# A gated delta-rule layer with its normalisation factor applied behind the output projection instead of ahead of it

## The reference, cut to what matters

```python
qkvz = hidden_states @ W_qkvz
conv = _silu(sum((xp[:, j:j + Tv, :] * conv_w[:, j] for j in range(CONV_K))))
# recurrence over time, per batch element and value head:
S = S * a_t[..., None, None]
err = jnp.einsum('bhkv,bhk->bhv', S, k_t)
v_new = (v_t - err) * b_t[..., None]
S = S + k_t[..., None] * v_new[..., None, :]
o = jnp.einsum('bhkv,bhk->bhv', S, q_t)
# behind it:
og = o * _silu(z)
og = og * jax.lax.rsqrt(jnp.mean(og * og, axis=-1, keepdims=True) + EPS) * norm_weight
return og.reshape(Bv, Tv, VDIM) @ W_out
```

## Time and profile before

| | us |
|---|---|
| median of 3 runs | 1351.96 |
| lowest, highest | 1344.74, 1357.4 |
| the profiled execution's own time | 1348.03 |
| its span (first to last instruction) | 1346.0 |
| busy PE, DVE, ACT, POOL | 1203.4, 924.2, 829.4, 744.7 |

### The profile page before, as it was taken

How to read it: one execution, slowest core, us unless ns; L and a number is a source line. 1 busy time by engine, 2 the same in 40 slices (tenths; PEclk the granted TensorE clock), 3 DMA queues, 4 the chain that set the end, 5 groups by cost and what they waited for, 6 DMA issues and landing times. The chain is left out here.

```text
span 1346.0 us, 30471 instructions
## 1 busy us (share of the span) xinstructions
PE 1203.4 (89%) x10744; PEld 1019.1 (76%) x10744; DVE 924.2 (69%) x2304; ACT 829.4 (62%) x2289; POOL 744.7 (55%) x1187
## 2 busy tenths in 40 slices
PE   7888998999999999999999999999998787997886
PEld 6787787787878888878877888878877676765654
DVE  6886877787878787887778787878772423325663
ACT  6335666666667676766666767667675535217773
POOL 2285756667676758585857667676757301112201
PEclk9776999999999999999999999999997869999997
DMA  4214041413121222214040403121123120001000
GB/s 168 74 38 106 6 104 7 105 24 87 31 80 35 75 41 71 53 58 103 7 107 5 106 20 91 27 83 36 36 41 108 30 94 1 0 27 41 2 9 24
DMA packets 143430, 72.82 MB, mean 54 GB/s; under 512 B 116744, under 2 KB 132624, under 8 KB 141360
## 3 DMA queue, kind: packets, MB, share of 16 engines
q1 hardware_dynamic: 143280, 70.89, 20.7%
HBM read 57.06 MB, written 13.78 MB: 53 GB/s over the span
## 5 line engine op out<-in xcount | busy, mean ns | idle before, releaser
L1011 POOL TENSOR_TENSOR tmp<-Dm,Tn 64x31 f32<-64x31 f32 (+15 forms) x496 | 262.4, 529 | 89.4 <-DMA Dm<-blk_in_scratch 54.1
L1014 POOL TENSOR_TENSOR Tn<-Tn,tmp 64x31 f32<-64x31 f32 (+15 forms) x496 | 285.4, 575 | 38.9
L823 DVE SCALAR_TENSOR_TENSOR cv<-bank,cw,cv 128x255 f32<-128x255 f32 (+2 forms) x384 | 155.2, 474 | 78.0 <-ACT cv L629 78.0
L987 POOL TENSOR_TENSOR ro<-ss,mhalf 128x4 f32<-128x4 f32 x64 | 65.1, 1017 | 250.1 <-ACT junk L691 214.0
L823 DVE SCALAR_TENSOR_TENSOR cqk<-bank,cw,cqk 128x255 f32<-128x255 f32 (+2 forms) x384 | 154.9, 473 | 7.5 <-ACT cqk L629 7.5
L454 PE MATMUL bank<-wo,OTs 128*128 128x256 f32 x512 | 138.6, 405 | 10.8 <-ACT OTs L722 10.8
L883 DVE SCALAR_TENSOR_TENSOR BP<-bank,cj,E 128x512 f32<-128x512 f32 (+1 forms) x256 | 142.8, 611 | 2.7 <-DVE cj L868 0.5
L691 ACT ACTIVATE junk<-og 128x129 f32<-128x129 f32 x256 | 79.9, 312 | 97.3 <-issue 80.6
L887 DVE TENSOR_TENSOR R<-Vs,bank 128x256 f32<-128x256 f32 x64 | 27.0, 421 | 141.9 <-PE bank L420 138.3
L454 PEld LDWEIGHTS bank<-wo,OTs 128*128 128x128 f32 x512 | 93.1, 197 | 25.8 <-ACT OTs L722 14.2
L699 ACT ACTIVATE ogn<-og,ro 128x128 f32<-128x128 f32 x256 | 81.9, 398 | 29.5 <-POOL ro L987 29.5
(11 more groups left out here) (210 smaller groups left out, 3492.7 us busy)
## 6 DMA issues: line engine op xcount, KB each, us to landing
rvz<-in_L_attn_W_qkvz SPq DMA_DIRECT2D x16, 512.0 KB, 5.0
x<-alpha_scratch SPq DMA_DIRECT2D x8, 1024.0 KB, 6.4
alb<-alpha_scratch SPq DMA_DIRECT2D x7, 1024.0 KB, 6.4
rqk<-in_L_attn_W_qkvz SPq DMA_DIRECT2D x16, 256.0 KB, 2.6
wo<-in_L_attn_W_out SPq DMA_DIRECT2D x16, 256.0 KB
blk_in_scratch<-BP SPq DMA_DIRECT2D x256, 16.0 KB, 1.5
tinv_scratch<-Tn SPq DMA_DIRECT2D x32, 128.0 KB, 2.1
tinv_t_scratch<-Tt SPq DMA_DIRECT2D x32, 128.0 KB, 2.2
```

The costliest lines, as they stand in the source:

```text
L823: nc.vector.scalar_tensor_tensor(d, bk[:, t * T:(t + 1) * T - s], cw[p][:, first + t, TAPS - 1 - s:TAPS - s], d, ALU.mult, ALU.add).then_i ...
L1011: pool_step_done(nc.gpsimd.tensor_tensor(t, Dm[:, j, j + 1:BLK].unsqueeze(2).broadcast_to([SLOTS, r, c]), Tn[:, j, 0:c].unsqueeze(1).broad ...
L1014: pool_step_done(nc.gpsimd.tensor_tensor(Tn[:, j + 1:BLK, 0:c], Tn[:, j + 1:BLK, 0:c], t, ALU.subtract), kh * NTS + 2 * j + 4)
```

## The change

1. The scaling `act_ogn` and its tile are gone. PE turns og itself. The projection writes each value head's product to its own half of the PSUM bank, for one block of 128 tokens at a time (c = 0, 1), so it is done in two rounds through the same bank; `dve_acc` takes a round with two instructions of 256 columns, each acc = product x ro + acc. The second round of the projection waits for the first round's accumulation. `ro` is now waited for by `dve_acc`.
2. The order of a step is written anew on PE, ACT and DVE.
3. The second layer: the last residual, statistics and norm of the first layer's end move from the block's boundary into the second layer's loop (k = 1, 3, 5), the first v product moves behind the first scores, and the value products are placed between turns.

```diff
             def pe_ot(kh, p, b, scaled):
-                wait(nc.tensor, "ogn", at(kh, b, 4, 4))
+                wait(nc.tensor, "og", at(kh, b, 2, 2))
...
             def pe_f(kh, p, b, c):
...
+                wait(nc.tensor, "acc", at(kh, b, 4, 2 * c))
                 for h in range(R):
-                    last = nc.tensor.matmul(bF[:, c * D:(c + 1) * D], OTs[:, h, c, :], wo[p][:, h, :],
-                                            start=(h == 0), stop=(h == R - 1))
-                if c == 1:
-                    last.then_inc(sem("f"), 1)
+                    last = nc.tensor.matmul(bF[:, h * D:(h + 1) * D], OTs[:, h, c, :], wo[p][:, h, :], start=True, stop=True)
+                last.then_inc(sem("f"), 1)
...
                 else:
+                    pe_ot(*last, 2 * (now + 2))
                     pe_solve(kh, p, b, 0)
                     pe_behind_solve(kh, b)
+                    pe_f(*last, 0)
                     if vt:
-                        pe_vt(*vt, now - 1)
+                        pe_vt(*vt, now)
...
                     pe_before_ot(kh, b)
-                    pe_ot(*last, 2 * (now + 3))
+                    pe_f(*last, 1)
                     pe_solve(kh, p, b, 2)
...
-                    pe_f(*last, 0)
-                    pe_f(*last, 1)
...
-            def act_ogn(kh, p, b):
...
+            def dve_acc(kh, p, b, c):
+                wait(nc.vector, "f", at(kh, b, 2, c + 1))
+                wait(nc.vector, "ro", at(kh, b, 1, 1))
+                a = acc[:, NC * b + c, :]
+                for h in range(R):
+                    wait(nc.vector, "acc", at(kh, b, 4, c * R + h))
+                    nc.vector.scalar_tensor_tensor(a, bF[:, h * D:(h + 1) * D], ro[b % 2][:, c * R + h:c * R + h + 1], a,
+                                                   ALU.mult, ALU.add).then_inc(sem("acc"), 1)
...
                 if not merges(b):
+                    dve_acc(*last, 0)
                     dve_r2(kh, p, b)
...
+                    if taps is taps_qk and not merges(b):
+                        dve_acc(*last, 1)
...
                 else:
+                    act_ots(*last)
                     act_y(kh, p, b, 0)
                     if vt:
                         act_vs(*vt)
-                    act_ogn(*last)
...
                     act_y(kh, p, b, 1)
-                    act_ots(*last)
...
-                res_ffn(B - 1)
-                dve.wait_ge(sem("res0b"), B)
```

More of the change, by code:

```diff
@@ L443, in pe_ot @@
                         n = h * NC + c
[L444 removed]
+                        last = nc.tensor.transpose(bOT[:, n * P:(n + 1) * P], og[b % 2][:, c, h, 0:DK], ident)
                 last.then_inc(sem("ot"), 1)
@@ L595, in pe_step @@
                     pe_solve(kh, p, b, 1)
-                    if vt:
-                        pe_vt(*vt, now)
+                    if last:
+                        pe_f(*last, 1)
                     pe_solve(kh, p, b, 2)
@@ L1313, in _ @@
                 pe_ot(NKH - 1, 1, B - 1, 2 * NG)
[L1314 to L1317, removed]
+                for m in range(2, HT):
                     pe_gate_up(0, m)
+                    if m < 4:
+                        pe_f(NKH - 1, 1, B - 1, m - 2)
                 pe_ln_turn(2)
@@ L1796, in _, with first_v @@
             def _(act):
[L1797 to L1808, removed]
+                for m in range(KC):
+                    act.wait_ge(sem("first_mm"), 2 + 2 * m)
+                    nc.scalar.activation(kp[:, m, 0:T], bank[5 - 2 * m][:, 0:T], ACT.Copy).then_inc(sem("first_act"), 1)
+                def first_v():
+                    act.wait_ge(sem("first_mm"), 5)
+                    act.wait_ge(sem("v10"), 1)
+                    for c in range(NC):
+                        for par in range(2):
+                            last = nc.scalar.activation(v1_out(0, c, 0, NH1, par), v1_in(bank[6][:, c * D:(c + 1) * D], par), ACT.Copy)
+                    last.then_inc(sem("first_act"), 1)
                 def exponents(n):
@@ L1848, in _ @@
                 for m in range(KC):
[L1849 to L1854, removed]
+                    for kind, bk in zip("qk", (4 + 2 * m, 5 - 2 * m)):
+                        product(bank[bk][:, 0:T], kind, m, slice(0, T)).then_inc(sem("first_mm"), 1)
                 pe.wait_ge(sem("first_dve"), 1)
-                pe.wait_ge(sem("first_act"), 2)
+                pe.wait_ge(sem("first_act"), KC)
                 def scores(n):
@@ L1946, in _ @@
                         pieces(k)
-                    if k == 1:
+                    if k == 0:
                         pe.wait_ge(sem("first_dve"), KC)
-                        pe.wait_ge(sem("first_act"), KC + 1)
+                        for c in range(NC):
+                            last = product_v(bank[6][:, c * D:(c + 1) * D], c, 0, D)
+                        last.then_inc(sem("first_mm"), 1)
+                    if k == 5:
+                        pe.wait_ge(sem("attn"), 1)
                         ln_turn(pe, 2, B - 1, (6, 6))
@@ L1955, in _ @@
                     if 0 <= k - 1 < NG:
-                        for j in range(GR):
+                        for j in range(2):
                             turned(GR * (k - 1) + j)
@@ L1959, in _ @@
                         values(k - 2)
-                        if k % 2 == 1:
-                            spread((k - 2) // 2)
+                    if 0 <= k - 1 < NG:
+                        for j in range(2, GR):
+                            turned(GR * (k - 1) + j)
+                    if 0 <= k - 2 < NG and k % 2 == 1:
+                        spread((k - 2) // 2)
                     if k >= 6 and (k - 6) % 4 == 0:
```

81 lines of the change are left out of this document (39 added, 42 removed).

## The result

| | before | after |
|---|---|---|
| median, us | 1349.78 (4 runs, 1344.74 to 1357.4) | 1496.37 (4 runs, 1492.65 to 1497.15) |
| profiled execution: its time, its span | 1348.03, 1346.0 | 1495.59, 1493.5 |
| mean granted clock of PE | 0.948 | 0.911 |

The ratio is 1.1075, with a 95% interval of 1.1017 to 1.1134. The forecast was 1485, in a range of 1400 to 1590.

A forecast was written before the change was run, and what follows sets the result against it. It took a loop through PE and DVE (z, Gram, solves, R2, taps) to set the plain step. 1348.0 + 108 (plain and merging steps) + 2 (last heads) + 28 (clock) - 4 (second layer) = 1482, put at 1485 us; range 1400 to 1590.

The forecast's parts named there:

- The loop: Plain steps: later solve 1 and a second accumulation round between the taps add 2.7 us in b = 3, 4.2 in b = 2.
- the signs named ahead: Plain steps of 16 to 18 us, PE idle over 3 us ahead of z, merging steps about as before, granted clock under 1.00.
- Merging steps: Behind merge stage 3 the projection's second round replaces `vt`: +0.4 us for each of two, +0.8 a head.
- The clock: Two 3.5 us PE idle times a head, one swallowed by waits: one short clock fall, 2 us a head, +28.
- its bound of +182: Upper bound of the low-clock cost, from a range of 0 to 13 us a head.
- The last two heads: The last two of 16 heads, outside the 14 with q, k and Gram work in plain steps: +2 us, between 0 and +4.
- Second layer: Last residual out of the boundary and v product behind the scores: -4 us, between 0 and -7.
- 1 (PE's pauses come back): PE is the bound and regains its 43.1 us of waits for the scaled output in plain steps: 1305 us, chance 0.07.
- 2: Delays half overlap, b = 2 delayed no more than b = 3, no clock fall: 1401 us, chance 0.16.
- 3: The clock stays low: both falls of a head last 13 us, 1639 us, or one of two, 1560; chance 0.13.

The follow-up runs named there:

- e8: The change with eight idle matmuls ahead of z in plain steps, one ahead of merge stage 2 and two ahead of stage 3: 1430.36 us, 1.0633.
- e7: e4 with the change's PE and ACT order in plain steps alone, accumulations staying behind gating: 1381.12 us, 1.0259.
- e9: e4 with DVE's second BP group of the plain steps moved from ahead of the taps to behind the taps of v: 1338.29 us, 0.9931.
- e1: The change with eight matmuls writing to an unused PSUM bank added ahead of z in the 28 plain steps: 1450.35 us, 1.0778.
- e5: The kernel before with only part 3 of the change, the second layer's: 1331.97 us, 0.9909.
- e4: The kernel before's order without the scaling, factor applied behind the projection, two PSUM banks, second layer as in the change: 1295.68 us, 0.9643.
- e6: e4 with the change's PE and ACT order in merging steps alone, R2 ahead of all four accumulations on DVE: 1364.58 us, 1.0146.
- e2: The change with the second accumulation round of plain steps behind the taps of v instead of ahead of them: 1456.3 us, 1.0839.
- e3: The change with the old order put back in plain steps, still one bank, both accumulations behind gating: 1398.55 us, 1.0403.

## Why the forecast was right, and where its terms were not

**The loop** (solve 1, R2, taps, z): right. Forecast +2.7 in b = 3 and +4.2 in b = 2; with the clock taken out (e8) they are 16.4 - 13.7 = 2.7 and 18.2 - 13.8 = 4.4. Its parts hold one by one: solve 1 later by 2.2 in b = 3 (e7) for 2.1 and by 3.6 in b = 2 (e8) for 3.25, second round 1.00 for 0.95, first round hidden, the first projection round waiting for OTs (0.62 and 1.66 us). The loop is confirmed from the other side by e9, whose steps b = 3 are 0.77 us shorter for the 0.87 taken out. Of the signs named ahead, the steps of 16 to 18 us and the merging steps as before did not come: the plain ones took mostly 18.9 to 21 us and the merging ones 17.9 to 19.8, and by e8 most of that is the clock's.

**Merging steps**: +0.8 was the right size (0.8 in b = 0 and 0.1 in b = 1, e8). I gave it to the longer projection round behind stage 3; I read it as the waits of 0.43 and 0.82 ahead of stages 2 and 3, as `vt` covers less; e8 fills them and keeps their length.

**The clock: mis-sized.** The step was "of two such idle times the one inside the plain steps is followed by waits that swallow it", 2 us a head, +28. Filling the pauses gave back 66 (e8), 4.7 a head. Both idle times of each head brought a fall, 24 of 24 between 190 and 1130 us of the trace. Behind the one inside the plain steps z and Gram took 6.31 us for 3.64, and they are in the loop, so nothing swallowed it; behind the one ahead of the merging step they took 5.2. The pauses in merging steps brought further falls in about half of the heads, which were not in the sum; e8 against e1 puts 20 us on them. The forecast's own bounds are also uneven: its upper end of 1560 takes 13 us for one of the two falls, where its bound of +182 has it for both.

**The last two heads: missed**, -24 for +2. There the change has neither the waits for the scaled output (10.8 us in six waits before, of 3.09 and 4.04 the longest) nor their low clock. Granted clock 0.80 before, 0.96 after:

```profile
998.00:1134.00 136.00, 110.61 (x952) 95.31 (x951) 45.96 (x108) 69.90 (x208) 48.65 (x78) 0.80 0.23 62
```

```profile
1184.00:1296.00 112.00, 91.63 (x952) 79.32 (x951) 54.55 (x130) 60.74 (x173) 48.77 (x79) 0.96 0.26 74
```

I had the 13 us of the earlier trace rows at hand and read it as a price the change might pay, not as one that the kernel before was paying. Part of the 24 is chance: the same code took 128.2 in e5's trace, for 136.0; e4, which has no scaling either, took 107.8.

**Second layer**: -14 in the trace and -12 in e5, for -4. I priced the boundary alone. The larger part lies in the loop: PE's waits for probT in it fell from 18.7 us to 8.5, as the value products stand between the turns.

**Rivals.** 1 (PE's pauses come back): its sum came out in e4, 1296 for 1305, but not its place. Of the 52 us by which e4's trace is shorter than before, the heads with full steps give 11, the last two heads 28 and the second layer 13; in a plain step there was little to win, as the prediction said (0.4 us at most). 2 failed on b = 2, delayed more than b = 3. 3 failed: in the change's middle heads each low stretch lasts 3 to 7 us and not 13.

The split of the whole: e4 is 200 us faster than the change. The plain order is 85 of that (e7) and the merging order 69 (e6). The remaining 46 I put on the two accumulation rounds through one bank, of which e2 gives 40 back. That the three add up was not run, and they overlap: some 29 of the 69 (2.1 us in 14 heads) come from both rounds of accumulation standing behind R2 in e6, of which the change has one there.

## What to carry to other kernels

Find the loop through all engines that sets a step, and ask of each moved piece whether it lands inside; e4 and the change do the same products and accumulations, with 200 us between them. Taking a wait off the bound engine buys nothing when something else delays what the other engine waits for. A new pause on PE can cost its length and then the low clock behind it, so it should be priced from trace rows with the clock of what follows, and the kernel before should be searched for the same cost already being paid.

## What the runs showed of the hardware

- Adding matmuls made the kernel faster: 8 more in each plain step and 3 in each merging step (e8), 66 us less.
- The length of a pause alone does not tell whether the clock falls. Of the pauses ahead of z, those of 1.02 us (e4) brought no fall in 25, those of 1.88 (e3) 10 in 25, those of 2.32 brought 24 in 25 in e2 and only 15 in 25 in e7, and those of 3.23 (the change) 24 in 24. In e2, e7 and the change a fall made z and Gram take 4.9 to 6.5 us for 3.64. Two pauses of 0.65 and 0.82 us around merge stages of 16 small products stood ahead of a window of 7 us at 0.51 (e6).
- Two accumulations of 256 columns into the same tile, the second waiting for the first, took 1.00 us; four that alternate between two tiles took 1.65, 0.41 each for 0.50. The Trainium skill (VectorE: DVE Perf Modes, "The DRAIN you can't avoid") measured eight copies with and without semaphores between them and found that the semaphore cost nothing extra; here the dependent form took 0.09 us more each. The two forms also differ in the banks read, so the wait alone isn't shown to be the cause.
